# Scattering the normalised rows straight from SBUF at the head of the experts' stage

## The reference, cut to what matters

```python
x = x + _L0_xattn_ref(_layernorm(x), ctx_1024, ...)      # ends with the feed-forward
x = x + _L0_ffn_ref(_layernorm(x), gate_w, W1, W2, W3)   # the experts
x = x + _L1_xattn_ref(_layernorm(x), ctx_1024, ...)
x = x + _L1_ffn_ref(_layernorm(x), ...)

def _L0_ffn_ref(x, gate_w, W1, W2, W3):
    scores = xf @ gate_w.T
    expert_weights, expert_indices = jax.lax.top_k(scores, 2)
    expert_weights = jax.nn.softmax(expert_weights, axis=-1)
    mid = jax.nn.silu(x @ W1[e].T) * (x @ W3[e].T)       # H = 896, for the chosen e
    y = sum over the two of (mid @ W2[e].T) * expert_weights
```

## Time and profile before

| | us |
|---|---|
| median of 3 runs | 1382.69 (1382.04 to 1382.87) |
| the profiled execution, its own time | 1381.46 |
| its span, first to last instruction | 1379.7 |
| PE busy | 1068.9 (77%) |
| DVE busy | 938.7 (68%) |
| ACT busy | 611.2 (44%) |
| POOL busy | 434.6 (32%) |

### The profile page before, as it was taken

The page is one execution under the profiler, slowest core; times in us unless marked ns, Lnnn a source line. Parts: engine busy times, 40 slices in busy tenths (PEclk is TensorE's granted clock), DMA queues, the critical chain, the costliest instruction groups (busy, mean ns, idle before and its releaser), DMA issues. The chain is left out here.

```text
span 1379.7 us, 26090 instructions
## 1 busy us (share of the span) xinstructions
PE 1068.9 (77%) x9362; PEld 728.5 (53%) x9362; DVE 938.7 (68%) x2598; ACT 611.2 (44%) x1228; POOL 434.6 (32%) x605
## 2 busy tenths in 40 slices
PE   4988778984799401899999999953587774999998
PEld 2655554542688401677877778741243432554554
DVE  5587887983377511788888888833777743777776
ACT  2376666763554001566656666512456560000000
POOL 4267754435166371121111111136343100000010
PEclk9699999998899655999999999985689996999999
DMA  7344345330233326466666665334322211100000
GB/s 207 107 120 103 104 109 154 94 94 6 88 105 128 108 91 252 174 239 213 207 227 231 240 230 207 131 117 125 97 76 79 62 38 57 36 24 31 24 8 16
DMA packets 127396, 164.25 MB, mean 119 GB/s; under 512 B 13075, under 2 KB 106022, under 8 KB 124326
## 3 DMA queue, kind: packets, MB, share of 16 engines
q1 hardware_dynamic: 123686, 153.41, 34.2%
q0 software_dynamic: 3584, 9.18, 2.0%
HBM read 117.01 MB, written 45.35 MB: 118 GB/s over the span
## 5 line engine op out<-in xcount | busy, mean ns | idle before, releaser
L1888 PE MATMUL moe_ps_u<-moe_x_hl,moe_up_hl 128*128 128x256 f16 x1932 | 226.2, 276 | 40.2 <-DVE moe_up_hl L1964 31.7
L1888 PEld LDWEIGHTS moe_ps_u<-moe_x_hl,moe_up_hl 128*128 128x128 f16 x1932 | 184.4, 99 | 82.1 <-DVE moe_up_hl L1964 38.2
L2137 PE MATMUL mix_ps_e<-wr_hl,mix_u_hl 128*128 128x512 f16 x768 | 172.3, 380 | 0.0
L2014 POOL CAST moe_mid_hl<-moe_mid 128x256 f16<-128x256 f32 x161 | 68.6, 426 | 312.9 <-DVE moe_mid L1979 312.9
L1964 DVE SCALAR_TENSOR_TENSOR moe_up_hl<-moe_up_in,moe_up_hl 128x512 f16<-128x512 f32 x161 | 105.2, 687 | 54.2 <-ACT moe_up_hl L1937 54.2
L547 ACT ACTIVATE dec_probs<-dec_ps_t 128x768 f32<-128x768 f32 (+1 forms) x128 | 117.2, 916 | 51.5 <-PE dec_ps_t L446 50.1
L2249 DVE SCALAR_TENSOR_TENSOR mix_acc<-mix_ps_e,mix_shares,mix_acc 128x256 f32<-128x256 f32 x256 | 110.4, 477 | 38.9 <-PE mix_ps_e L2137 38.5
L1937 ACT ACTIVATE moe_up_hl<-moe_up_in 128x512 f16<-128x512 f32 x161 | 99.1, 619 | 61.9 <-DMA moe_up_in<-in_moe_w 61.9
L2137 PEld LDWEIGHTS mix_ps_e<-wr_hl,mix_u_hl 128*128 128x128 f16 x768 | 74.8, 98 | 83.3 <-issue 0.8
L1900 PE MATMUL moe_ps_y<-moe_down_hl,moe_mid_hl 128*128 128x256 f16 x966 | 109.1, 273 | 0.0
L1205 DVE TENSOR_REDUCE mem_neg_m<-mem_ps_s 128x2 f32<-128x512 f32 x128 | 82.3, 686 | 31.4 <-PE mem_ps_s L1049 30.6
(11 more groups left out here) (276 smaller groups left out, 1906.1 us busy)
## 6 DMA issues: line engine op xcount, KB each, us to landing
moe_up_in<-in_moe_w SPq DMA_DIRECT2D x23, 1792.0 KB, 7.3
moe_down_in<-in_moe_w SPq DMA_DIRECT2D x23, 896.0 KB, 4.7
dec_q_dram<-dec_q_hl SPq DMA_DIRECT2D x48, 128.0 KB, 2.2
dec_k_dram<-dec_k_hl SPq DMA_DIRECT2D x48, 128.0 KB, 2.0
dec_q_st<-dec_q_dram SPq DMA_DIRECT2D x64, 96.0 KB, 2.6
dec_k_st<-dec_k_dram SPq DMA_DIRECT2D x64, 96.0 KB, 2.6
xs<-zeros SPq DMA_DIRECT2D x8, 736.0 KB
moe_x_in<-xs SPq DMA_DIRECT2D x23, 256.0 KB, 4.4
```

Of the source, the lines that this page charges most:

```text
L1888: mm = nc.tensor.matmul(bank[:, m, :], up_hl[t.slot][:, w, m, dc, f * P:(f + 1) * P], x_hl[t.slot][:, x, dc, :], start=(dc == 0 and w == x ...
L2014: nc.gpsimd.tensor_copy(mid_hl[t.slot][:, HI, f, :], mid[:, f, :]).then_inc(mid_hi, 1)
L2137: mm = nc.tensor.matmul(ps_e[fill % RING][:, :, :], u_hl[t.slot][:, r, dc, k * P:(k + 1) * P], wr_hl[:, m, dc, 2 * q:2 * q + 2, :], start= ...
```

## The change

The rows no longer go through DRAM. A tensor `normed_rows` of all eight batches is allocated in SBUF for the whole program; DVE writes the normalised rows of `feed_forward` into it in place of the ring `res_n`, and the gate's transposes read it. The stores to `hm`, the loads to `route_rows` and their semaphores are gone. The 32 indirect DMAs leave `route` and stand first in POOL's list of `experts`. There SP's list is written anew: the loads of matrices for tiles 0 and 1 come first, the load of rows for tile 0 waits for `scattered`, and from tile 1 on the rows are loaded right behind the down matrix of the same tile. For tile 0, DVE makes all seven low parts of the up matrices ahead of the rows' low part.

```diff
--- before.py
+++ after.py
@@ feed_forward, sync, vector @@
-                    if older.within():
-                        sp.wait_ge(res_n_done, TT * (older.n + 1))
-                        sp.dma_start(out_normed[older.n], res_n[older.slot][:, :, :]).then_inc(res_n_stored[older.slot], 16)
...
-                        if d.before(2):
-                            dve.wait_ge(res_n_stored[d.slot], 16 * d.turn)
-                            dve.wait_ge(r_turned, d.n - 1)
                         for k in range(TT):
-                            nc.vector.tensor_scalar(res_n[d.slot][:, k, :], res[d.slot][:, k, :], mv_o[d.slot][:, k, 0:1],
+                            nc.vector.tensor_scalar(normed_rows[:, d.n * TT + k, :], res[d.slot][:, k, :], mv_o[d.slot][:, k, 0:1],
@@ route @@
-            @block.sync
-            def _(sp):
-                for b in range(BATCHES):
-                    sp.dma_start(rows[:, b * TT:(b + 1) * TT, :], normed[b]).then_inc(rows_loaded, 16)
-
...
-                pool.wait_ge(rows_loaded, 16 * BATCHES)
-                pool.wait_ge(zeroed, 16 * BATCHES)
-                for k in range(2):
-                    pool.wait_ge(slots_done, k + 1)
-                    for t in range(NT):
-                        nc.gpsimd.indirect_dma_start(xs[:, :], bass.IndirectOffsetOnAxis(ap=slots[:, k, t:t + 1], axis=0),
-                                                     rows[:, t, :], None).then_inc(scattered, 16)
-                pool.wait_ge(scattered, 16 * 2 * NT)
@@ experts, sync @@
+                def load_rows(t):
+                    if t.n == 0:
+                        sp.wait_ge(scattered, 16 * 2 * NT)
+                    if t.before(2):
+                        sp.wait_ge(turned, t.n - 1)
+                    sp.dma_start(x_in[t.slot][:, :, :], xs_t[t.n]).then_inc(x_loaded[t.slot], 16)
+
                 def step(t):
                     new, ahead, old = t.plus(2), t.plus(3), t.plus(-1)
+                    if t.n == -1:
+                        load_rows(t.plus(1))
                     if new.within():
...
                         sp.dma_start(down_in[new.slot][:, :, :], w2[e]).then_inc(down_loaded[new.slot], 16)
+                    if new.within() and new.n > 0:
+                        load_rows(new)
                     if ahead.within():
                         e = sp.value_load(tile_expert[0:1, bass.ds(ahead.n, 1)], min_val=0, max_val=E - 1)
-                        if ahead.before(2):
-                            sp.wait_ge(turned, ahead.n - 1)
-                        sp.dma_start(x_in[ahead.slot][:, :, :], xs_t[ahead.n]).then_inc(x_loaded[ahead.slot], 16)
                         if ahead.before(2):
                             sp.wait_ge(up_split, HC * (ahead.n - 1))
@@ experts, vector @@
                     if nxt.within():
                         mid_low(nxt, HC - 1)
+                    if new.n == 0:
+                        for f in range(0, HC, 2):
+                            up_low(new, f)
                     if new.within():
                         dve.wait_ge(x_hi, new.n + 1)
...
                     for f in range(0, HC, 2):
-                        if new.within():
+                        if new.within() and new.n > 0:
                             up_low(new, f)
@@ experts, gpsimd @@
             def _(pool):
+                pool.wait_ge(zeroed, 16 * BATCHES)
+                for k in range(2):
+                    for t in range(NT):
+                        nc.gpsimd.indirect_dma_start(xs[:, :], bass.IndirectOffsetOnAxis(ap=slots[:, k, t:t + 1], axis=0),
+                                                     rows[:, t, :], None).then_inc(scattered, 16)
+
                 def step(t):
```

More of the change, by code:

```diff
@@ L1330, in _, with feed_forward @@
                         add_outputs(mixed)
-def feed_forward(nc, c, rows, x, w1_hl, b1, w2_hl, b2, gain, shift, gate, out, out_normed, logits, xs, zeroed):
+def feed_forward(nc, c, rows, x, w1_hl, b1, w2_hl, b2, gain, shift, gate, out, normed_rows, logits, xs, zeroed):
     with ExitStack() as ctx:
@@ L1398, in step @@
                 def step(t):
-                    old, older = t.plus(-2), t.plus(-4)
+                    old = t.plus(-2)
                     if t.within():
@@ L1621, in _, with route @@
                 pipeline(pool, step, 1, 2)
-def route(nc, c, logits, normed, xs, weights, slots, tile_expert, zeroed):
+def route(nc, c, logits, weights, slots, tile_expert):
     with ExitStack() as ctx:
@@ L1652, in route @@
         gap, exped, both = sb("gap", [P, NT]), sb("exped", [P, NT]), sb("both", [P, NT])
-        rows = sb("rows", [P, NT, D])
         ps_p = ctx.enter_context(nc.psum_tensor("route_ps_p", [P, BANK], F32))
@@ L1657, in route @@
         made, exps, chose, counted, stepped = sem("made"), sem("exps"), sem("chose"), sem("counted"), sem("stepped")
[L1658 removed]
+        gap_done, slots_done = sem("gap_done"), sem("slots_done")
         with nc.Block() as block:
[L1661 to L1664 removed]
             @block.tensor
@@ L1777, in _, with experts @@
                                         pattern=[[1, P]], channel_multiplier=-1).then_inc(made, 1)
-                pool.wait_ge(rows_loaded, 16 * BATCHES)
-                pool.wait_ge(zeroed, 16 * BATCHES)
-                for k in range(2):
-                    pool.wait_ge(slots_done, k + 1)
-                    for t in range(NT):
-                        nc.gpsimd.indirect_dma_start(xs[:, :], bass.IndirectOffsetOnAxis(ap=slots[:, k, t:t + 1], axis=0),
-                                                     rows[:, t, :], None).then_inc(scattered, 16)
-                pool.wait_ge(scattered, 16 * 2 * NT)
-def experts(nc, c, xs, w13, w2, tile_expert, ys, matrices):
+def experts(nc, c, rows, slots, xs, zeroed, w13, w2, tile_expert, ys, matrices):
     with ExitStack() as ctx:
@@ L1808, in experts @@
         E, HC = w2.shape[0], w2.shape[2]
+        NT = slots.shape[2]
         x_in, x_hl = ring(sb, "x_in", [P, TT, D]), ring(sb, "x_hl", [P, 2, DC, SEQ], F16)
@@ L1816, in experts @@
         ps_y = ring(ps, "ps_y", [P, TT, D])
+        scattered = sem("scattered")
         x_loaded, up_loaded, down_loaded = ring(sem, "x_loaded"), ring(sem, "up_loaded"), ring(sem, "down_loaded")
@@ L2387, in program @@
         ctx_hl = dram("ctx_hl", [2, D, TOKENS], F16)
-        xa, hm = dram("xa", rows), dram("hm", rows)
+        xa = dram("xa", rows)
+        normed_rows = sb("normed_rows", [P, BATCHES * TT, D])
         logits = sb("logits", [P, BATCHES * TT, E])
@@ L2401, in program @@
             feed_forward(nc, c, resident, i["x"], w1_hl, i["bf1"], w2_hl, i["L0_xattn_bf2"], i["L0_xattn_g3"], i["L0_xattn_be3"],
-                         i["gate"], xa, hm, logits, xs, zeroed)
-        route(nc, c, logits, hm, xs, shares, slots, tile_expert, zeroed)
+                         i["gate"], xa, normed_rows, logits, xs, zeroed)
+        route(nc, c, logits, shares, slots, tile_expert)
         wc_hl, ws_hl, cent_hl = parts(ctx, "wc_hl", [D]), parts(ctx, "ws_hl", [D]), parts(ctx, "cent_hl", [routed])
         wr_hl = parts(ctx, "wr_hl", [routed, D])
-        experts(nc, c, xs, i["moe_w13"], i["moe_w2"], tile_expert, ys,
+        experts(nc, c, normed_rows, slots, xs, zeroed, i["moe_w13"], i["moe_w2"], tile_expert, ys,
                 [([i["mem_wc"]], flat(wc_hl)), ([i["centroids"]], flat(cent_hl)), ([i["mix_ws"][0], i["mix_ws"][1]], flat(ws_hl)),
```

8 lines of the change are left out of this document (3 added, 5 removed).

## The result

| | before | the change |
|---|---|---|
| median of 19 runs, us | 1381.95 | 1370.62 |
| lowest to highest, us | 1374.94 to 1388.23 | 1365.78 to 1379.36 |
| ratio to before | | 0.9924 (0.9908 to 0.9941) |
| profiled execution: span, us | 1379.7 | 1366.7 |

The ratio is a gain of 10.5 us (8.2 to 12.7); the forecast was 11.0. Places in two traces are compared by their distance from the copy of `logits` that ends the feed-forward (473.12 before, 472.66 now), which takes out what earlier stages happened to do.

The account below looks back on a forecast made before the run. Bound by the serial stretch between `route` and `experts`; later start, scatter pace, DVE contention and a shorter way out put the first product at 535.72 against 546.69, so 1382.69 - 11.0 = 1371.7 us, range 1368.0 to 1375.7.

Parts of the forecast that it names:

- What bounds: Border of `route` and `experts`: 21.5 us from last scatter start to first product, mostly loading and splitting matrices, not needing the scatter.
- this hole: The 15th profile slice, 483 to 517 us, with PE doing nothing: serial, so whatever leaves it leaves the kernel.
- Later start: First scatter now waits for the barrier after DVE's last routing row: 487.94 us, 2.19 late.
- Pace: Scatter's indirect DMAs: 1.31 us from first to second, then 37.92 us for 30, 1.264 each.
- port lock: Rival: each low part holds POOL off for its whole length, 4.8 us in place of 0.8, total 1375.7; 12%.
- DVE beside POOL: Seven low parts beside the scatter each lengthen an indirect DMA by 0.11 us, 0.8 us in all.
- the rule it cites: Trainium skill: two-SBUF-input DVE instructions contend only with GpSimd instructions reading SBUF; two-port-mode ones block GpSimd for their whole length.
- The drain: POOL's queue drain of 2.675 us and the barrier no longer stand between scatter landing and SP's load of rows.
- Stall behind the loads: Rival: POOL's descriptors find no room while matrices load, scatter stands still 11 us, gain cancels, 1382.7; 4%.
- Rows late: Rival: rows queued behind the down matrix land late in each of 21 steps, 21 us lost, 1392.7; 3%.
- Clock: First 24 products of `experts`: PE's clock may rise earlier, up to 2.0 us more gain; within the main case's range.

Follow-up runs that it names:

- repeat: The changed kernel run again unaltered, beside a version with three additions: ratio to before 0.9925 (0.9897 to 0.9954), median 1371.28 us.
- experiment 1: Changed kernel with rows in SBUF, but scatter, SP's order and DVE's low parts as before the change: ratio to before 1.0009 (0.9990 to 1.0027).
- experiment 4: Changed kernel with tile 0's seven low parts held until the scatter landed; one run within 1369.9 to 1375.3 us, first to last scatter start 39.49 us.
- experiment 5: Changed kernel plus unread DVE work beside the scatter (8 two-input operations, 12 copies, 12 `tensor_scalar`); one run within 1369.9 to 1375.3 us, scatter 42.2 us.
- experiment 6: Changed kernel plus 84 unread PE products from the 26th scatter landing on; one run within 1369.9 to 1375.3 us, first product at 63.93 us.

## Why the prediction was right

The forecast was 1371.7 by a gain of 11.0; 1370.62 and 10.5 (by the ratio) were measured. The mechanism was the one forecast. Step by step, in us; the first and the last row are distances from the copy of `logits`:

| step | forecast | profile | repeat |
|---|---|---|---|
| first scatter | 14.82 | 14.54 | 14.52 |
| first to last start | 40.03 | 39.81 | 40.86 |
| last start to SP's load of rows | 2.50 | 2.44 | 2.45 |
| load to transposes | 2.67 | 2.68 | 2.74 |
| transposes to first product | 2.58 | 2.61 | 2.60 |
| first product | 62.60 | 62.08 | 63.17 |

- *The total.* That the first product is within 0.6 us of the forecast in both profiles is in part luck: in the first the start came 0.3 us earlier than forecast, the scatter's first gap was 0.2 longer and the low parts cost 0.5 less, and in the repeat the low parts cost 0.6 more.
- *What bounds.* That the gain is in this hole is borne out by experiment 1 (no change of time with the trip through DRAM gone) and by the 23 tiles behind the first product, 373.8 us against 373.9.
- *Later start.* 2.19 us forecast, 1.91 measured. DVE's last row shrank from 0.43 to 0.17 us, as the row beside it had suggested.
- *Pace.* I had taken 1.31 us from the first to the second from memory attention; it was 1.55, as in `route` before (1.54). The first is 1.24 long with DVE idle too (experiment 4), so this row, which I had also read as a hint of the port lock, was no hint.
- *DVE beside POOL.* 0.8 us by seven times the nearest row. Measured 0.3 to 1.5 in seven kernels with low parts beside the scatter, two of which had 14 more DVE operations there (length from first to last start above 39.49); the cause is shown by experiments 4 and 5. The size was right by luck, as a middle value, and not by the working: beside the seven low parts alone, one or three of the indirect DMAs are lengthened, each by 0.32 to 0.54 and not by 0.11. The row behind the 0.11 was not near in kind either: it stood beside one-input operations. The full port lock, 4.8 us, did not come. The prediction laid it to the half of the rule it cites that speaks of a two-port mode; the low parts have two inputs, so it is the copies and `tensor_scalar` of experiment 5 that test that half, and no indirect DMA stood still for the length of one there either.
- *The drain.* That it would leave the path was right. The prediction did not say where it would go: it moved to the end of `experts`, where it ends 8 us before the barrier opens.
- *Stall behind the loads.* DMAs landed in up to 8.2 us and POOL was not slowed: excluded by experiment 4, where the loads ran and all took 0.96.
- *Rows late.* Excluded by the landings of 5.9 us at most.
- *Clock.* The extra gain from an earlier rise, up to 2.0 us, did not come: 4.65 us for the first 24 products against 4.81. In experiment 6, with work on PE ahead of the rows, they took 2.78, close to the 2.85 that the prediction had for the upper level.

## What to carry to other kernels

Where a scatter must end before its readers begin, put what the readers need besides it (loads of weights and their splits) into the same block ahead of the wait, and let the queue that needs the scatter wait for it, not the barrier. Look at what is left behind the wait instruction by instruction, since here four operations in the wrong order were 2.4 of 9.2 us, and the step behind it had some 6 us more to give once its matrices, its table and PE's clock were seen to in the idle time. Taking a trip through DRAM out was worth nothing by itself here, because it was hidden.

## What the runs showed that I had not expected

- POOL's queue drain costs 2.7 to 3.1 us once in the block in which the scatter was issued, even 370 us after the last of its indirect DMAs (3.135 us at 896.5, the last issued at 527.01). The same two blocks without the scatter drain in 0.39 us (`route`, in the change) and 0.51 (`experts`, before). Other blocks without indirect DMAs drain in 0.04 to 1.4 us, and `memory_attention`, with 48 of them, in 4.2.
- DVE operations and indirect DMAs hold each other off, by little, and the kind decides who pays (experiment 5): beside two-input operations an indirect DMA of 0.96 us becomes 1.14 to 1.5 and DVE loses next to nothing; beside copies and `tensor_scalar` it becomes 1.04, once 1.21, and some of DVE's take up to 0.65 us in place of 0.43. DVE's row of 23 numbers took 0.43 us beside the first scatter and takes 0.17 now. Beside the 0.69 us `tensor_reduce` of memory attention no indirect DMA took over 1.04 us.
- With the DMA engines full (share 1.01) indirect DMAs are issued at the same 1.264 us.
